# Two attention stages on one core: how the sums of probabilities are split between GpSimd and VectorE

## What is computed

```
x = x + L0_attn(layernorm(x))            # 16 heads, 1024 keys
x = x + L0_xattn(layernorm(x), context)  # 16 heads of 64, 6404 keys
x = x + L0_ffn(layernorm(x))
x = x + L1_attn(layernorm(x))            # 16 heads of 8, 1024 keys
x = x + L1_xattn(layernorm(x), context)  # 8 heads of 64, 6404 keys
x = x + L1_ffn(layernorm(x))

sim  = einsum('bhid,bhjd->bhij', q, k) * scale
attn = softmax(sim, axis=-1)
out  = einsum('bhij,bhjd->bhid', attn, v) ... @ Wo + bo
```

## Time and profile before

| what | us |
|---|---|
| median of 3 runs (4997.2 to 5010.37) | 5000.62 |
| the profiled execution, own time | 5001.35 |
| its span in the profile | 4999.5 |
| TensorE busy | 4609.8 (92%) |
| GpSimd busy | 3024.6 (60%) |
| VectorE busy | 2551.6 (51%) |
| ScalarE busy | 1873.6 (37%) |

### The profile page before, as it was taken

One profiled execution on the slowest core, in us unless ns is written; L12 is line 12 of the kernel. 1 busy time (PEld: TensorE's weight loads), 2 busy tenths in 40 slices (PEclk: granted clock), 3 DMA queues, 4 the chain that ended last, 5 costly groups with the idle time before them and its releaser, 6 DMA issues. The chain is left out here.

```text
span 4999.5 us, 71279 instructions
## 1 busy us (share of the span) xinstructions
PE 4609.8 (92%) x25712; PEld 2300.0 (46%) x25712; DVE 2551.6 (51%) x2948; ACT 1873.6 (37%) x2082; POOL 3024.6 (60%) x2371
## 2 busy tenths in 40 slices
PE   7999699999999999999999989499789999999979
PEld 3555344444444444454444437244344454444436
DVE  4554555555555555555555432466454555555442
ACT  2333134444444444444444433144224444443433
POOL 3555067777877777787777960000037787777960
PEclk9999599999999999999999989699679999999989
DMA  0000000000000000000000000100000000000001
GB/s 12 5 5 2 22 2 1 2 2 2 2 1 3 1 3 1 3 2 1 2 1 2 1 11 28 52 12 11 23 2 1 2 2 1 2 1 1 1 9 30
DMA packets 31856, 33.53 MB, mean 7 GB/s; under 512 B 7137, under 2 KB 23090, under 8 KB 31538
## 3 DMA queue, kind: packets, MB, share of 16 engines
q1 hardware_dynamic: 28626, 24.39, 1.7%
q10 hardware_dynamic: 2912, 4.92, 0.4%
HBM read 25.63 MB, written 3.67 MB: 6 GB/s over the span
## 5 line engine op out<-in xcount | busy, mean ns | idle before, releaser
L401 POOL TENSOR_TENSOR c_SUM<-c_SUM,c_PR 128x512 f32<-128x512 f32 x2016 | 2619.7, 1331 | 689.6 <-ACT c_PR L490 688.5
L563 DVE TENSOR_REDUCE c_MX<-c_XB 128x2 f32<-128x1024 f32 (+1 forms) x1180 | 1397.1, 1184 | 1268.5 <-PE c_XB L689 1266.5
L490 ACT ACTIVATE c_PR<-c_S 128x1024 f32<-128x1024 f32 (+1 forms) x1224 | 1251.6, 1023 | 1971.3 <-PE c_S L736 1889.3
L752 PE MATMUL c_O<-c_PR,c_V 128*64 128x512 f32 (+1 forms) x4896 | 1329.6, 622 | 0.0
L736 PE MATMUL c_S<-c_SH,c_ONE 64*128 64x512 f32 x2448 | 488.1, 394 | 0.0
L736 PEld LDWEIGHTS c_S<-c_QH,c_KHM 64*128 64x128 f32 x1728 | 162.6, 185 | 635.6 <-ACT c_PR L490 314.7
L752 PEld LDWEIGHTS c_O<-c_PR,c_V 128*64 128x64 f32 (+1 forms) x4896 | 243.4, 135 | 428.0 <-issue 316.0
L736 PE MATMUL c_S<-c_QH,c_KHM 64*128 64x512 f32 x1728 | 427.0, 490 | 8.1 <-ACT c_PR L490 5.2
L490 ACT ACTIVATE a_PR<-a_S 128x1024 f32<-128x1024 f32 x256 | 262.0, 1023 | 453.6 <-PE a_S L736 453.1
L563 DVE TENSOR_REDUCE a_MX<-a_XB 128x2 f32<-128x1024 f32 x246 | 301.2, 1224 | 249.8 <-PE a_XB L689 138.2
L689 PE MATMUL c_XB<-c_KHM,c_QH 64*128 64x512 f32 x1632 | 353.0, 427 | 72.7 <-DVE c_MX L563 72.7
(11 more groups left out here) (207 smaller groups left out, 4387.5 us busy)
## 6 DMA issues: line engine op xcount, KB each, us to landing
f_W<-in_L_w SPq DMA_DIRECT2D x34, 256.0 KB, 2.6
CTX<-in_ctx ACTq DMA_DIRECT2D x24, 192.0 KB, 4.3
a_KS<-scratch_k SPq DMA_DIRECT2D x16, 96.0 KB
a_QS<-scratch_q SPq DMA_DIRECT2D x16, 96.0 KB
scratch_q<-rot_qh SPq DMA_DIRECT2D x2, 512.0 KB, 4.5
scratch_k<-rot_kh SPq DMA_DIRECT2D x2, 512.0 KB, 6.3
c_WQ<-in_L_xattn_Wq SPq DMA_DIRECT2D x12, 64.0 KB, 1.8
c_WO<-in_L_xattn_Wo SPq DMA_DIRECT2D x12, 64.0 KB, 1.8
```

Source lines behind the costliest of these rows:

```text
L401: pool.tensor_tensor(SUM[half][0:kp, h, :], SUM[half][0:kp, h, :], tile[0:kp, h, :], ALU.add)\
L490: act.activation(PR[u % BUFS][0:kp, :, :].rearrange("p h q -> p (h q)"), S[u % 2][0:kp, :], ACT.Exp)\
L563: dve.tensor_reduce(MX[:, q, :, c], bank[:].rearrange("p (h k) -> p h k", h=2)[:, :, 0:m], AX.X, ALU.max)\
L752: last = pe.matmul(O[ROWS[h], :], V[pair.par][0:kp, t, ROWS[h]], PR[u % BUFS][0:kp, h, :], start=t == 0, stop=t == TILES - 1)
```

## The change

The adds are divided by columns instead of by tiles. GpSimd adds columns 0 to 415 of both heads of every tile in one instruction (128x2x416), VectorE columns 416 to 511 (128x2x96), both into `SUM`. `SUMV` and the merge are gone. `probabilities` and job D now wait for both engines. In the same edit the table of side jobs is rewritten: in half 0 YA and YB follow D at steps 7 and 8 (before 8 and 10), and the 13 jobs V stand in steps 9 to 21, one in each (before in 12, 14, 17, 19, ... 42); in half 1 each job K stands one step ahead of its first maximum (before three). The steps of the maxima and a0's table of side jobs are as they were. `group` is 1, so a group is a step.

```diff
+        self.split = 416
+        self.group = 1
-            wanted[0] = [(0, ("Q", 1)), (6, ("D", 1)), (8, ("YA", 1)), (10, ("YB", 1))]
-            wanted[0] += [(12 + 2 * c + c // 2, ("V", c)) for c in range(self.chunks)]
-            wanted[1] = [(0, ("Q", 0)), (6, ("D", 0)), (8, ("YA", 0)), (10, ("YB", 0))]
+            must[0] = {0: ("Q", 1)}
+            must[1] = {0: ("Q", 0)}
             for c in self.order:
-                first = min(step for step, _, _, chunk in self.maxima[1] if chunk == c)
-                wanted[1].append((max(first - 3, 1), ("K", c)))
+                first = min(g for g, _, _, chunk in self.maxima[1] if chunk == c)
+                must[1][first - 1] = ("K", c)
+            fill[0] = [("D", 1), ("YA", 1), ("YB", 1)] + [("V", c) for c in range(self.chunks)]
+            fill[1] = [("D", 0), ("YA", 0), ("YB", 0)]
...
+            g = 4 if self.group == 2 else 6
+            for job in fill[half]:
+                while g in at:
+                    g += 1
+                at[g] = job
...
-        dve = [] if packed else [2, 3, *range(12, final, 9)] if wide else [2, 3]
-        self.adds = [[t for t in range(self.tiles) if t not in dve], dve]
...
+        def add(eng, added, columns, pair, half, t):
+            if t == 0:
+                return
+            kp = plan.tile_keys(t)
+            tile = PR[(half * TILES + t) % BUFS]
+            out = SUM[half]
+            eng.wait_ge(p_done, plan.step(pair.p, half, t) + 1)
...
+            eng.wait_ge(added, plan.added(pair.p, half, t - 1))
+            eng.tensor_tensor(out[0:kp, :, columns], out[0:kp, :, columns], tile[0:kp, :, columns], ALU.add)\
+               .then_inc(added, 1)
...
-                        for t in mine:
-                            add(pair, half, t)
-                        merge(pair, half)
+                        for t in range(TILES):
+                            add(pool, pool_added, slice(0, SPLIT), pair, half, t)
...
-                            if b_t in plan.adds[0]:
-                                act.wait_ge(pool_added, 2 * plan.added(0, owner.p, b_half, b_t))
-                            else:
-                                act.wait_ge(dve_added, plan.added(1, owner.p, b_half, b_t))
+                            n = plan.added(owner.p, *divmod(was, TILES))
+                            act.wait_ge(pool_added, n)
+                            act.wait_ge(dve_added, n)
...
+                            def sums(t):
+                                if packed is None and 0 <= t < TILES:
+                                    add(dve, dve_added, slice(SPLIT, HALF), pair, half, t)
...
+                            maxima(0)
...
+                            for job in side_jobs(half, group, end):
                                 side(pair, job, end)
+                            sums(t if GROUP == 2 else t - 1)
+                            maxima(2 if GROUP == 2 else 1)
```

More of the change, by code:

```diff
@@ L1 @@
+from collections import Counter
 from contextlib import ExitStack
@@ L62, in __init__ @@
         for half in range(2):
[L63 to L68, removed]
+            at = dict(must[half])
+            g = 4 if self.group == 2 else 6
[3 more added lines that the diff above has]
+                at[g] = job
+            at[final] = ("M", 1 - half)
@@ L69, in __init__ @@
+            assert max(at) == final and len(at) == len(must[half]) + len(fill[half]) + 1
             self.side.append(at)
@@ L236, in absent, with side_jobs, maxima_at, steps_of @@
             return pair is not None and pair.first and job[0] in ("D", "YA", "YB") and job[1] == 1
-        def side_jobs(half, t, end):
-            job = plan.side[half].get(t)
+        def side_jobs(half, group, end):
+            job = plan.side[half].get(group)
             return [] if job is None or (end and plan.of_next(job)) else [job]
-        def maxima_at(half, t, behind, end):
+        def maxima_at(half, group, place, end):
             if end and half == 1:
                 return []
-            return [(i, q, c) for i, (step, b, q, c) in enumerate(plan.maxima[half]) if (step, b) == (t, behind)]
+            return [(i, q, c) for i, (g, at, q, c) in enumerate(plan.maxima[half]) if (g, at) == (group, place)]
+        def steps_of(group):
+            return range(group * GROUP, min((group + 1) * GROUP, TILES))
+        def add(eng, added, columns, pair, half, t):
[5 more added lines that the diff above has]
+            eng.wait_ge(p_done, plan.step(pair.p, half, t) + 1)
+            if t == 1:
+                if not pair.first:
+                    if half == 0:
+                        eng.wait_ge(side_done, plan.job(pair.p - 1, ("D", 0)) + 1)
+                    else:
+                        eng.wait_ge(side_done, plan.job(pair.p, ("D", 1)) + 1)
+                one = PR[half * TILES % BUFS]
+                eng.tensor_tensor(out[:, :, columns], one[:, :, columns], tile[:, :, columns], ALU.add).then_inc(added, 1)
+                return
+            eng.wait_ge(added, plan.added(pair.p, half, t - 1))
+            eng.tensor_tensor(out[0:kp, :, columns], out[0:kp, :, columns], tile[0:kp, :, columns], ALU.add)\
+               .then_inc(added, 1)
         LEAD = [("side", j) for j in plan.lead if j[0] == "Q"]
@@ L376, in _ @@
                 pool.wait_ge(filled, FILLS)
[L377 to L389, removed]
-                        else:
[L391 to L404, removed]
-                    pool.wait_ge(pool_added, 2 * plan.added(0, pair.p, half, mine[-1]))
-                    pool.wait_ge(dve_added, plan.added(1, pair.p, half, plan.adds[1][-1]))
-                    for h in range(2):
-                        pool.tensor_tensor(SUM[half][:, h, :], SUM[half][:, h, :], SUMV[half][:, h, :], ALU.add)\
-                            .then_inc(merged, 1)
                 def copy_v(pair):
@@ L498, in period @@
                     for half in range(2):
-                        for t in range(TILES):
-                            probabilities(pair, half, t)
-                            for job in side_jobs(half, t, end):
+                        for group in range(GROUPS):
+                            for t in steps_of(group):
+                                probabilities(pair, half, t)
+                            for job in side_jobs(half, group, end):
                                 side(pair, job, end)
-                            if t == LAG - 1:
+                            if LAG - 1 in steps_of(group):
                                 if half:
@@ L793, in _ @@
                 if packed is None:
[L794 removed]
+                    pe.wait_ge(pool_added, plan.added(pairs - 1, 1, TILES - 1))
+                    pe.wait_ge(dve_added, plan.added(pairs - 1, 1, TILES - 1))
                 pe.wait_ge(evac, 2 * pairs)
```

103 lines of the change are left out of this document (49 added, 54 removed).

## The result

The changed kernel takes 5154.68 us, the median of four runs (5140.94 to 5156.14), against 5000.57 before: 1.0299 times as long (95% interval 1.0276 to 1.0321). The direction and the range of the prediction hold; the predicted 5240 was too high, since the change costs 154 us and not 239. The profiled execution took 5155.45 us.

What follows compares the result with a forecast made beforehand. TensorE bounds c0 and c1, held by how soon VectorE has reduced a maximum. Terms 152 + 51 - 13 + 49 = 239 us on the profiled 5001.35 gave 5240 us, range 5110 to 5350.

Steps and rivals of the forecast that it cites:

- What bounds the kernel: In c0 and c1 TensorE bounds, held only by how soon VectorE has reduced a maximum; that wait is 100.7 us.
- P: Length of GpSimd's new 832-column add: 2.02 us, with bounds of 1.89 and 2.16.
- The held add: VectorE's small add, 0.35 us alone, stands still behind GpSimd's and ends about 0.22 us after it.
- S: Start of a step's exponential, from which the prediction counts times within the step.
- A: Steps with two maxima: the add between them delays the second, 1.5 us a step without cover; 152 us in all.
- B: Plain steps: a held add delays the next maximum, one stop in three plain steps; 128 stops of 0.4 us, 51 us.
- C: Gains and small things: last halves -12, merge and double adds gone -9, a0 +8; -13 us in all.
- A's standstill of 1.9 us: TensorE's stop before the second maximum, like job D in length; about 80 such steps without a side job.
- D: Clock falling to half after standstills: 80 steps x 0.36 x 1.7 us, 49 us, from nothing to 136.
- VectorE goes first: Rival: GpSimd's start moves behind VectorE's add, which then costs 0.35 us, hidden; 4980 to 5020, chance 0.10.
- Only the second maxima hurt: Rival: plain steps absorb their delay and the clock holds; 5140 us, chance 0.2.
- GpSimd falls behind: Rival: GpSimd's cycle passes 2.4 us, so it never idles in plain steps and each stretches; 5330 us, chance 0.15.

Runs made afterwards that it cites:

- first_old_table: Changed kernel with the old side-job table, and GpSimd waiting for VectorE's add of tile t-1 before tile t: 4954.5 us, 0.9903 times.

## Why the prediction was right, and where it was off

**What bounds the kernel** stood. The 154 us came mainly through the wait for the maxima and the clock that fell with it, and went with them. Only the last few us, in the kernels that have GpSimd second, hang on the ends of the stages.

**P, GpSimd's instruction.** Predicted 2.02 us, measured 1.97. The instruction's means over all sizes that ran are 1.12 us for 416 columns, 1.70 for 704, 1.97 for 832 and 2.24 for 960, where the first has some standstill in it: about 2.1 ns a column and 0.2 us fixed. The Trainium skill, "GPSIMD Engine Reference", section "Elementwise — side-by-side cycle accounting", led to an estimate of 1.80 us, which the runs contradict.

**The held add.** VectorE ends 0.21 us behind GpSimd (predicted 0.22). The mean of 1.5 us or more for the small add was wrong, 1.26: in a half the delay shifts VectorE's queue later, so it asks later and has less of GpSimd's instruction left to wait out. I had let every add ask at S+1.3; at 1377.77 this one asks at S+2.03. The second maximum of step 30 starts at S+3.27 and not at S+3.5.

**A and B**, 152 and 51 us, were the mis-sized terms. A, B and C together come to what the clock doesn't take: 154 - 56 = 98 us, where I had 190. Taken by halves, with half of each stretch of half clock off, those with maxima are 86 us longer in c0 and 27 in c1. That is A and B together: 113 us, where I had 203.
- In A the pair of steps costs 1.34 us and not 1.5, and step 2 of half 0, one of the four steps without cover, cost nothing: 5.87 us with the step that follows it, 6.02 before. Its add is the one of tile 1 and was not held.
- In B one stop costs 0.25 us, not 0.4: the plain steps with a stop take 2.63 us against 2.37, as the lag of 0.3 is less what the queue caught up. In half 0 there are five of them and not six.
- A's standstill of 1.9 us in every second maximum was the step that failed. In c0 and c1 of the changed kernel 12 standstills last 1.7 us or more, at most 1.76, and not 80; most of the others come in twos of 0.9 to 1.1 us. A held add delays the next one's request, and VectorE then waits for less. This is also why the wait for `c_MX` grew to 195.7 us and not to over 250.

**C**, -13. The last halves of c0 and c1 are 7.9 and 8.7 us shorter (predicted 6 each), and at the three stage ends job D comes 9 us earlier in all, as foreseen. The 112 us predicted for a last half, from GpSimd's pace, came near by luck: it takes 110.5 us in c1 at splits of 256, 352 and 416 alike, so GpSimd no longer sets the pace there. Against it a0's attention grew by 27 us where I had 8. Its step with job M grew by the predicted 0.5 us, and TensorE's wait for `a_NM` went from 5.7 to 13.2 us, which is those 8. The other 19 or so go with stretches of half clock: 12 of the 16 jobs D in a0 are followed by one, where 4 were before. Why it is more often was not tested. ScalarE's waits, which I had costed at nothing, cost nothing that can be seen: the profile puts 176.7 us of its idle time to VectorE's sums, but nearly all of it in steps with a side job or right behind one, and a V step still takes 3.45 us.

**D, the clock**, was the least sure term, 49 us, and came out at 41 in c0 and c1; no term had the 20 more in a0. That the size was about right is luck, since the count was not: I had 80 standstills of 1.9 us with a chance of 0.36 each. In c0 of the changed kernel 11 of the 12 long standstills are followed by half clock, and five twos of 0.9 to 1.1 us besides; job D goes before it as often as in the kernel before, ten times within c0 and c1. No run isolates what the clock alone costs, since each that cured the waits cured it too.

**The rivals.** *VectorE goes first* had 4980 to 5020 for a kernel that fell into that order by itself. It did not; made to by one wait, the kernel takes 4952, less than that rival's lower end: the two second maxima that I charged with up to 42 us cost nothing (6.02 us for steps 30 and 31, as before). What makes it faster than before is in part the same as in C, the last halves (-9.5 and -8.7 us). The ends of c0 and c1 are no part of it, because job D starts 7.8 and 5.9 us after the last exponential, where it was 5.9 and 5.75. The rest fits the whole-tile adds that no longer hold the maxima of half 1, whose steps 4 and 5 take 6.03 us together and not 7.62 (a job K has left them too; with the old table, in `first_old_table`, they take 6.75). *Only the second maxima hurt* gave 5140 and came nearer in number than my 5240, but by a cancellation: the clock did fall, and plain steps did cost. *GpSimd falls behind* didn't happen at 832 columns in the changed kernel.

## What to carry to other kernels

When an instruction of one engine stands still until one of another engine ends, first ask who gets there first, and only then how much each does: one wait that lets the short instruction go ahead of the long one turned a loss of 3% into a gain of 1%, with the same instructions. What the loser waits is the rest of the other's instruction, so a long merged instruction is dear for its neighbour even where it saves its own engine work; cut it, or put the held instruction behind everything that the bounding engine waits for. A held instruction costs nothing by itself: look for what is queued behind it.

## What the runs showed that I had not expected

- A wait that was added, on the idle engine, made the kernel 202 us faster (5154.68 to 4952.31) and nothing else was touched.
- Cutting GpSimd's instruction in two raised its busy time by 258 us over the changed kernel's 2316.0 and the kernel became 160 us faster.
- How unevenly the clock answers to a standstill. Of the 12 of 1.73 to 1.76 us in c0 of the changed kernel 11 were followed by half clock, 1.2 GHz: nine with matmul pairs of 0.63 us behind them (as at 1449.27 above), two, at 1133.83 and 1256.74, with 0.78 and 0.79 in the pair that ends the standstill. In c0 of the kernel before there are 12 of 1.26 to 1.31 us, one of them in the earlier trace rows, and none was followed by it without a job D between. But length alone doesn't decide. The kernel before has four standstills of 2.28 us, one in c0 and three in c1, and only the one that ends at 3847.30 was followed by half clock at once; twos of 0.9 to 1.1 us were followed by it five times in c0 of the changed kernel. And one of its 12 long ones was not, with the pairs behind it at 0.40:

```profile
1879.30 0.51 PE L679 MATMUL c_XB<-c_KHM,c_QH 64*128 64x512 f32 x2 [1.74 <-DVE c_MX L554]
...
1881.09 0.40 PE L726 MATMUL c_S<-c_QH,c_KLA 64*128 64x512 f32 x2
```
